# VectorE's three operations for the base row, from the fifth side group to the end of the tile's list

## The chip, the core and the metric

The kernel runs on one core of a Trainium2 chip. The metric is the device time of one execution in microseconds; less is better. The core has five engines, each with its own list of instructions and its own queue: TensorE (matrix products), VectorE, ScalarE, GpSimd, and SyncE, which here only issues DMA transfers. The lists are tied together by semaphores alone: an instruction waits for a count, and another one raises it when it has ended. No compiler orders the work; the order in each list is the order in the program.

## The reference

One transformer block on x of shape (4, 1024, 128) in float32:

```
x = x + ga * attention(layernorm(x) * (1 + ca) + sa)          # 16 heads of width 8
h = layernorm(x) * (1 + cb) + sb
probs = softmax(h @ router_w.T); p, idx = top_k(probs, 2)      # 8 experts
w = p / (p.sum(-1) + 1e-6)
x = x + gb * ((h @ expert[idx] + p) * w).sum over the two
```

The gates ga, gb and the shifts and scales come from a small table per batch. What matters here is the last line. It is computed as `base + gb * mixed`. `mixed` is the sum over all 8 experts of their output times a coefficient, which is 0 for the six not chosen. `base` is what remains: the row after attention, x1, plus gb times one number per token, `bias_w`, the sum of p times w over the two chosen experts.

## The kernel before

The 4096 tokens are 32 tiles of 128. Tiles 0 to 3 and 28 to 31 are written out, and a hardware loop of 12 rounds does two tiles a round, so tiles 4 to 27 are loop tiles; between an odd loop tile and the next even one lies the back edge. Counts of semaphores are numbers in the written-out tiles and come out of registers in the loop.

A tile t is built around the attention of tile t. TensorE computes scores in eight steps k = 0 to 7 (L801), ScalarE takes their exponentials into `probs` (L608), 16 of 128x1024 a tile, and TensorE multiplies these with the values two steps later (L819). The first operation of each step k is followed on TensorE by a side group, `side0` to `side7`, all of which share one PSUM bank, `ps_side`. They carry the other stages of other tiles, as a hand-written pipeline: layernorm and projections of tiles t+1 to t+3, the output projection and the second layernorm of tile t-1, and the router and experts of tiles t-2 and t-3. Since they share the bank, each group waits until VectorE has read what the group before it left. The ones around the change:

- `side5` (k=5) puts the products of experts 0 and 1 of tile t-2 into `ps_side`. VectorE weighs them with the router's coefficients into `weighted` (`c_weigh`, piece 0, L1264), the first weighting.
- `side6` (k=6) waits for that weighting, and transposes `xhat`, computes logits and the norms of the keys. VectorE answers with `norm_max`, `hT`, `c_logits` and `c_vals` (the reciprocal L1180 and `valsT` L1182).
- `side7` has experts 2 and 3, which VectorE weighs as piece 1, the second weighting, the last entry of VectorE's list for a tile.
- `side0` of the next tile waits for the second weighting, projects `valsT` and sums the flags. VectorE's list for a tile begins with `exact_maxima` (L1146), which loads a flag from SBUF into a register (L1149) and branches on it (L1150), and goes on with `c_x1`: x1 (L1187), its statistics (L1189, L1191), and `a_bounded` (L1144).
- `side1` waits for x1_done and bounded_done (`emptied0`) before it puts the third pair of experts in the bank.

`c_router_base` (L1242) is what the change moves: `pair_pw` (L1245, 128x2), `bias_w` (L1247, 128x1) and `base` (L1253, 128x128). Each waits for the one before it. `base` also waits for out_done of an earlier tile, and reads x1 out of one of two buffers; the next tile's `c_x1` writes that same buffer.

GpSimd has a list of its own: the two coefficients and their sum when the weights are known, `squares` of the projected queries and keys (L462), then `mix_eight` and `mix_two` for tile t-3: sums of 128x512 (L505), 128x256 (L507) and 128x128 (L511), the product with the gate (L519), and the addition of `base` (L525). For that last step it waits for base_done of tile t-3's row, which VectorE computed one tile earlier. ScalarE issues the store of the finished tile (L343) at the end of its list.

Of the kernel before, what the change touches and what calls it, by code (L numbers as in the profile page):

```python
# [51 lines left out]
def reached(eng, sem, count):  # L52

    if not isinstance(count, int) or count > 0:
        eng.wait_ge(sem, count)


def reached_apart(eng, sem, count, past, past_count):


    if not isinstance(count, int):
        count = eng.to_reg(count)
        eng.wait_ge(past, past_count)
    reached(eng, sem, count)


def spread(ap, axis, n):

    ap = ap.unsqueeze(axis)
    shape = list(ap.shape)  # L70
    shape[axis] = n
    return ap.broadcast_to(shape)


def adaln_block(nc, x, Wqkv, bqkv, Wo, bo, router_w, expert_w, c, wmod, out):
# [25 lines left out]
    with ExitStack() as ctx:  # L101
# [3 lines left out]
        def sem(name):  # L105
            return ctx.enter_context(nc.semaphore(name))
# [155 lines left out]
        ev = {n: sem(n) for n in names}  # L262
# [25 lines left out]
        def plus(eng, t, n):  # L288

            return t + n if isinstance(t, int) else eng.snap(t + n)  # L290
# [5 lines left out]
        def batch_of(eng, t):  # L296
            return t // TB if isinstance(t, int) else eng.snap(t // TB, min_val=0, max_val=B - 1)
# [777 lines left out]
        def _(dve):  # L1075
# [108 lines left out]
            def c_x1(ps, y1, ring):  # L1184
                reached(dve, ev["attn_proj_done"], y1)
                reached(dve, ev["x_gated_done"], y1)
                v.tensor_tensor(x1[:, ring, :], ps[:, 0:P], x_gated[:], ALU.add).then_inc(ev["x1_done"], 1)  # L1187
                reached(dve, ev["x1_done"], y1)
                v.bn_stats(stats2[:], x1[:, ring, :]).then_inc(ev["stats2_done"], 1)  # L1189
                reached_apart(dve, ev["stats2_done"], y1, x_rest, 16)  # L1190
                v.bn_aggr(moments2[:], stats2[:]).then_inc(ev["moments2_done"], 1)  # L1191
# [22 lines left out]
            def c_router_sorted(y1):  # L1214

                coef_before = plus(dve, y1, -1)
                reached(dve, ev["router_exp_done"], y1)
                reached(dve, ev["coef_done"], coef_before)
                v.tensor_reduce(router_sum[:], router_exp[:], AX.X, ALU.add).then_inc(ev["router_sum_done"], 1)
                reached(dve, ev["router_sum_done"], y1)  # L1220
                v.reciprocal(router_inv[:], router_sum[:]).then_inc(ev["router_inv_done"], 1)
                reached(dve, ev["router_inv_done"], y1)
                v.tensor_scalar(router_p[:], router_exp[:], router_inv[:], None, ALU.mult).then_inc(ev["router_p_done"], 1)
                reached_apart(dve, ev["router_p_done"], y1, x_rest, 16)
                v.max(top_p[:], router_p[:]).then_inc(ev["top_p_done"], 1)
# [16 lines left out]
            def c_router_base(y, y1, ring):  # L1242

                reached(dve, ev["pair_w_done"], y1)
                v.tensor_tensor(pair_pw[:], top_p[:, 0:2], pair_w[:], ALU.mult).then_inc(ev["pair_pw_done"], 1)  # L1245
                reached(dve, ev["pair_pw_done"], y1)
                v.tensor_tensor(bias_w[:], pair_pw[:, 0:1], pair_pw[:, 1:2], ALU.add).then_inc(ev["bias_w_done"], 1)  # L1247
                b = batch_of(dve, y)
                out_before = plus(dve, y1, -2)
                reached(dve, ev["bias_w_done"], y1)  # L1250
                reached(dve, ev["out_done"], out_before)
                gate = gates[:, b, :] if isinstance(b, int) else gates[:, bass.ds(b, 1), :].rearrange("p a d -> p (a d)")
                v.scalar_tensor_tensor(out=base[:, ring, :], in0=gate, scalar=bias_w[:], in1=x1[:, ring, :], op0=ALU.mult,  # L1253
                                       op1=ALU.add).then_inc(ev["base_done"], 1)

            def c_weigh(ps, y1, ring, piece):

                e0, e1 = PIECES[piece]
                mix_before = plus(dve, y1, -2)
                reached(dve, experts_done[piece], y1)  # L1260
                if piece == 0:
                    reached(dve, ev["coef_done"], y1)
                    reached(dve, ev["mix4_done"], mix_before)
                v.tensor_tensor(weighted[:, ring, e0:e1, :],  # L1264
                                ps[:, 4 * P - (e1 - e0) * D:4 * P].rearrange("p (e d) -> p e d", d=D),
                                spread(coef[:, e0:e1], 2, D), ALU.mult).then_inc(weighted_done[piece], 1)

            def gates_copied():
                dve.wait_ge(setup_pe, 5)
                step(v.tensor_copy(gates[:].rearrange("p b d -> p (b d)"), ps_side[:]))  # L1270
                assert step.n == SETUP_GATES
# [9 lines left out]
            def tile(t, parity, before, after):  # L1281
                at = {n: plus(dve, t, n) for n in range(-4, 5)}
                if isinstance(t, int) and t == 1:
                    dve.wait_ge(x_rest, 16)
                exact_maxima(t, at[1], parity)
                if before == 0:
                    a_norm_max(ps_side[:, P + NE:P + NE + 2 * J], 2)
                    a_hT(2, 3, 0)

                if after >= 1:  # L1290
                    reached(dve, ev["flags_done"], at[2])
                if before >= 2:
                    c_x1(ps_side, at[-1], parity)
                if after >= 1:
                    a_bounded(ps_side[0:1, P + R:P + R + 1], at[2], 1 - parity)

                if before >= 4:
                    c_weigh(ps_side, at[-3], parity, 2)
                if before >= 2:
                    c_x1hat(at[-1], parity)  # L1300
                if before:
                    c_save(t)

                if before == 0:
                    gates_copied()
                if before == 1:
                    weights_gated()
                if before >= 4:
                    c_weigh(ps_side, at[-3], parity, 3)
                if after >= 3:  # L1310
                    a_moments(at[3], at[4])
                if before >= 3:
                    c_router_sorted(at[-2])

                if before >= 2 and after >= 1:
                    reached(dve, ev["v_ps_done"], at[2])
                if before >= 2:
                    c_h2T(ps_side, at[-2], at[-1], parity)
                if before >= 2 and after >= 1:
                    a_values(ps_side[:, P:2 * P], at[2], 1 - parity)  # L1320
                if before >= 3:
                    c_router_weights(at[-2])

                if before < 2:
                    reached(dve, ev["v_ps_done"], at[2])
                if after >= 2:
                    a_qk(at[3])
                if before < 2:
                    a_values(ps_side[:, 2 * P:3 * P], at[2], 1 - parity)
                if after == 0:  # L1330
                    c_logits(ps_side, at[-1])
                if after >= 2:
                    a_qk_parts(at[2], at[3])
                if after >= 3:
                    a_xhat(at[3], at[4])
                if before >= 3:
                    c_router_base(at[-3], at[-2], 1 - parity)

                if before >= 3:
                    c_weigh(ps_side, at[-2], 1 - parity, 0)  # L1340
                if after == 0:
                    c_router_sorted(t - 1)
                    c_router_weights(t - 1)
                    c_vals(t)

                if after >= 2:
                    a_norm_max(ps_side[:, P + NE:P + NE + 2 * J], at[3])
                if after >= 3:
                    a_hT(at[3], at[4], 1 - parity)
                if before >= 2 and after:  # L1350
                    c_logits(ps_side, at[-1])
                if before and after:
                    c_vals(t)

                if after == 0:
                    c_x1(ps_side, t, 0)
                if before >= 3:
                    c_weigh(ps_side, at[-2], 1 - parity, 1)
                if after == 0:
                    c_x1hat(t, 0)  # L1360
                    c_router_base(t - 2, t - 1, parity)
                    c_h2T(ps_side[:, P:2 * P], t - 1, t, 2, own_ring=True)
# [222 lines left out]
```

## Time and profile before

| | |
|---|---|
| median of 3 runs | 575.02 us (574.36 to 576.14) |
| the profiled execution | 575.76 us, span 574.0 us |
| TensorE, matmul busy | 507.4 us (88%) |
| ScalarE busy | 489.5 us (85%) |
| VectorE busy | 374.4 us (65%) |
| GpSimd busy | 227.7 us (40%) |
| TensorE's granted clock, mean | 0.982 of 2.4 GHz |

The span runs from the first to the last instruction of the profiled execution; the execution's own time has a little around it. Busy shares are means over the whole. Matmuls are pipelined and their ends are modelled, so that neighbours overlap a little. In an order of time each line is a start, a duration, the engine (PE is TensorE, DVE VectorE, ACT ScalarE, POOL GpSimd; a q behind the name is the engine's queue), the line of the program and the operation; the square brackets give the idle time before it and what ended it.

### The profile page before, as it was taken

The numbers are of one execution on the slowest core, as the hardware profiler recorded it, in microseconds if no ns is written. First come the engines' busy times: TensorE is split into PE (matmuls) and PEld (weight loads), VectorE is DVE, ScalarE is ACT, GpSimd is POOL, SyncE is SP. The second block draws the span as 40 slices with busy tenths as digits, with TensorE's granted clock in tenths as the row PEclk, the third lists the DMA queues.
The fourth block names the chain that finished last, engine by engine and source line by source line (L and its number), as shares of the span: only waits on it lengthen the run. The fifth ranks groups of instructions, "written<-read, shape, count | busy, mean of one in ns | idle before, by whom it ended". The sixth has DMA issues, their size and how long they took to land.

```text
span 574.0 us, 19559 instructions
## 1 busy us (share of the span) xinstructions
PE 507.4 (88%) x6667; PEld 195.9 (34%) x6667; DVE 374.4 (65%) x1258; ACT 489.5 (85%) x574; POOL 227.7 (40%) x488
## 2 busy tenths in 40 slices
PE   6879899888888988888898888899888889988987
PEld 6523233323333332333333233333323333332326
DVE  4414566667777666777766677776667777666566
ACT  1378999888889888888988888898888899888975
POOL 1101323345454334545433444543344454334444
PEclk9688999999999999999999999999999999999999
DMA  5563323333223233322323332232333222333000
GB/s 113 150 176 85 90 73 97 94 95 86 73 70 87 74 95 94 85 71 72 86 76 95 94 82 70 76 83 78 95 93 83 69 78 83 81 99 97 21 22 19
DMA packets 83342, 48.25 MB, mean 84 GB/s; under 512 B 59608, under 2 KB 74084, under 8 KB 83300
## 3 DMA queue, kind: packets, MB, share of 16 engines
q1 hardware_dynamic: 68860, 43.30, 28.0%
q10 hardware_dynamic: 14440, 4.38, 3.5%
q8 instruction: 27, 0.44, 0.3%
q14 instruction: 15, 0.12, 0.1%
HBM read 32.78 MB, written 14.87 MB: 83 GB/s over the span
## 4 chain that ended last, share of the span: by engine, by line
PE 61%; DVE 17%; issue 10%; ACT 7%; DMA 2%; SPq 1%; DVEq 1%; ACTq 1%; POOL 0%; POOLq 0%
PE ps_attn L819 26%; PE ps_side L724 18%; PE ps_scores L801 13%; ACT probs L608 7%; DVE bias_w L1247 5%; DVE pair_pw L1245 2%; DVE qkT L1114 2%; DVE weighted L1264 2%; DVE xhat L1100 2%; DVE qk_parts L1123 1%; PE ps_side L747 1%; DMA bo_rows<-in_L_attn_bo_dram 1%; PE ps_scores L676 1%; PE ps_scores L722 1%; DVEq L1253 1%
## 5 line engine op out<-in xcount | busy, mean ns | idle before, releaser
L608 ACT ACTIVATE probs<-ps_scores 128x1024 f32<-128x1024 f32 x512 | 479.8, 1053 | 71.7 <-PE ps_scores L801 70.6
L819 PE MATMUL ps_attn<-probs,values 128*32 128x512 f32 x2048 | 273.5, 601 | 0.1
L801 PE MATMUL ps_scores<-query_stack,key_stack 32*128 32x512 f32 x1024 | 130.6, 498 | 12.8 <-issue 8.1
L801 PEld LDWEIGHTS ps_scores<-query_stack,key_stack 32*128 32x128 f32 x1024 | 49.9, 183 | 229.9 <-ACT probs L608 198.9
L454 POOL TENSOR_SCALAR var_eps<-moments 128x1 f32<-128x1 f32 x64 | 12.3, 192 | 217.8 <-DVE moments L1191 143.0
L724 PE MATMUL ps_side<-experts_in,h2T 128*32 128x256 f32 x896 | 72.3, 390 | 4.0 <-issue 0.9
L1264 DVE TENSOR_TENSOR weighted<-ps_side,coef 128x256 f32<-128x256 f32 x114 | 47.8, 419 | 37.6 <-PE ps_side L724 36.5
L819 PEld LDWEIGHTS ps_attn<-probs,values 128*32 128x32 f32 x2048 | 57.0, 110 | 25.4 <-DVE attn L1174 8.3
L724 PE MATMUL ps_side<-ident,xhat 128*32 128x128 f32 x240 | 13.0, 289 | 38.2 <-DVE weighted L1264 37.2
L505 POOL TENSOR_TENSOR mix<-weighted 128x512 f32<-128x512 f32 x29 | 37.1, 1279 | 3.7 <-ACT weighted L626 3.7
L456 POOL TENSOR_TENSOR rstd<-var_eps,minus_half 128x1 f32<-128x1 f32 x64 | 36.2, 566 | 5.4 <-POOL var_eps L454 0.2
L488 POOL TENSOR_SCALAR coef<-expert_ids,top_idf,pair_w 128x8 f32<-128x8 f32 x30 | 12.2, 406 | 64.7 <-DVE pair_w L1240 64.7
L1187 DVE TENSOR_TENSOR x<-ps_side,x_gated 128x128 f32<-128x128 f32 x31 | 9.0, 292 | 39.7 <-PE ps_side L761 38.5
L1247 DVE TENSOR_TENSOR bias_w<-pair_pw 128x1 f32<-128x1 f32 x30 | 31.0, 1032 | 1.0
L724 PEld LDWEIGHTS ps_side<-experts_in,h2T 128*32 128x32 f32 x896 | 19.1, 108 | 33.4 <-issue 32.6
L1180 DVE RECIPROCAL sums_inv<-sums 128x128 f32<-128x128 f32 x31 | 29.3, 944 | 1.8 <-DMA attnT<-a_scr 1.8
L462 POOL TENSOR_TENSOR squares<-qkT 128x256 f32<-128x256 f32 x32 | 22.8, 712 | 13.0 <-DVE qkT L1114 8.9
L1174 DVE COPY attn<-ps_attn 128x512 f32<-128x512 f32 x31 | 21.4, 692 | 7.6 <-PE ps_attn L819 6.8
L1137 DVE TENSOR_REDUCE norm_max<-ps_side 128x1 f32<-128x32 f32 x31 | 6.0, 192 | 28.4 <-PE ps_side L724 28.4
L1253 DVE SCALAR_TENSOR_TENSOR base<-gates,bias_w,x 128x128 f32<-128x128 f32 x30 | 19.1, 635 | 6.5 <-DVE bias_w L1247 6.3
L1204 DVE TENSOR_SCALAR h2T<-ps_side,mod_tab 128x128 f32<-128x128 f32 x31 | 12.7, 410 | 14.6 <-PE ps_side L747 14.1
L507 POOL TENSOR_TENSOR mix<-mix 128x256 f32<-128x256 f32 x29 | 21.1, 727 | 2.3
(185 smaller groups left out, 547.6 us busy)
## 6 DMA issues: line engine op xcount, KB each, us to landing
key_stack<-k_scr SPq DMA_DIRECT2D x128, 128.0 KB, 2.8
query_stack<-q_scr SPq DMA_DIRECT2D x125, 64.0 KB, 2.2
q_scr<-qk_parts SPq DMA_DIRECT2D x94, 64.0 KB, 1.7
k_scr<-qk_parts SPq DMA_DIRECT2D x64, 64.0 KB, 1.7
a_scr<-attn ACTq DMA_DIRECT2D x120, 18.0 KB
sums<-a_scr SPq DMA_DIRECT2D x31, 64.0 KB, 2.1
attnT<-a_scr SPq DMA_DIRECT2D x31, 64.0 KB, 2.2
out_dram<-out_all ACTq DMA_DIRECT2D x28, 64.0 KB, 2.7
```

Source lines behind the costliest of these rows:

```text
L456: g.tensor_tensor(out_[:], var_eps[:], minus_half[:], ALU.pow).then_inc(ev[done_out], 1)
L462: g.tensor_tensor(flat, src, src, ALU.mult).then_inc(ev["squares_done"], 1)
L505: g.tensor_tensor(mix4[:], weighted[:, ring, 0:4, :], weighted[:, ring, 4:8, :], ALU.add).then_inc(ev["mix4_done"], 1)
L608: nc.scalar.activation(probs[:, k % RING, g, :], ps_scores[:, slot(k, g), :], ACT.Exp, scale=SCALE)\
L724: mm = nc.tensor.matmul(dst[q:q + 32, :], stationary[:, q:q + 32], moving, start=True, stop=True, tile_position=(0, q))
L801: mm = nc.tensor.matmul(out_, key_stack[p0:p0 + 32, parity, 2 * k:2 * k + 2, :].rearrange("p j r -> p (j r)"), query_stack[p0:p0 + 32, par ...
L819: mm = nc.tensor.matmul(ps_attn[q:q + 32, :], values[:, parity, g, k, :], probs[:, k % RING, g, h * HALF:(h + 1) * HALF], start=(k == 0), ...
L1174: v.tensor_copy(attn[:].rearrange("p j r -> p (j r)"), ps_attn[:]).then_inc(ev["attn_saved"], 1)
L1180: v.reciprocal(sums_inv[:], sums[:]).then_inc(ev["sums_inv_done"], 1)
L1247: v.tensor_tensor(bias_w[:], pair_pw[:, 0:1], pair_pw[:, 1:2], ALU.add).then_inc(ev["bias_w_done"], 1)
L1253: v.scalar_tensor_tensor(out=base[:, ring, :], in0=gate, scalar=bias_w[:], in1=x1[:, ring, :], op0=ALU.mult, op1=ALU.add).then_inc(ev["bas ...
L1264: v.tensor_tensor(weighted[:, ring, e0:e1, :], ps[:, 4 * P - (e1 - e0) * D:4 * P].rearrange("p (e d) -> p e d", d=D), spread(coef[:, e0:e1 ...
```

## The change

VectorE's call of `c_router_base` in a tile is taken out from before the first weighting. In tiles 3 to 30 it stands behind the second weighting now, at the end of the tile's list. In tile 31 (`after == 0`) it stands behind the first weighting, in front of the router's work for tile 30. As `base` reads the buffer that the next tile's x1 is written to, `c_x1` gets a wait for base_done. The call for the last but one row in tile 31 (`c_router_base(t - 2, t - 1, parity)`) stays where it is. No other engine's list changes.

```diff
             def c_x1(ps, y1, ring):
                 reached(dve, ev["attn_proj_done"], y1)
                 reached(dve, ev["x_gated_done"], y1)
+                base_before = plus(dve, y1, -2)
+                reached(dve, ev["base_done"], base_before)
                 v.tensor_tensor(x1[:, ring, :], ps[:, 0:P], x_gated[:], ALU.add).then_inc(ev["x1_done"], 1)
...
                 if after >= 3:
                     a_xhat(at[3], at[4])
                 if before >= 3:
-                    c_router_base(at[-3], at[-2], 1 - parity)
-
-                if before >= 3:
                     c_weigh(ps_side, at[-2], 1 - parity, 0)
                 if after == 0:
+                    c_router_base(at[-3], at[-2], 1 - parity)
                     c_router_sorted(t - 1)
...
                 if before >= 3:
                     c_weigh(ps_side, at[-2], 1 - parity, 1)
+                if before >= 3 and after:
+                    c_router_base(at[-3], at[-2], 1 - parity)
                 if after == 0:
                     c_x1hat(t, 0)
                     c_router_base(t - 2, t - 1, parity)
```

## Rows read from the trace of the kernel before

**Rows 1.** Busy time in two windows: window, length, then busy time of each engine.

```profile
304.05:320.57 16.52, 14.92 (x211) 5.41 (x211) 11.88 (x39) 14.91 (x18) 7.26 (x15) 1.00 0.31 84
320.57:337.57 17.00, 15.04 (x210) 5.51 (x211) 11.73 (x39) 15.07 (x18) 7.37 (x15) 1.00 0.30 81
```

**Rows 2.** List of waits: who waited for whom: total us, times, longest us.

```profile
PE ps_side L724 <- DVE weighted L1264: 38.4, 26, 1.5
```

**Rows 3.** TensorE's order of time: start us, duration us, operation.

```profile
300.61 0.64 PE L724 MATMUL ps_side<-experts_in,h2T 128*32 128x256 f32 x8
...
302.04 0.51 PE L801 MATMUL ps_scores<-query_stack,key_stack 32*128 32x512 f32 x4
304.05 0.43 PE L724 MATMUL ps_side<-ident,xhat 128*32 128x128 f32 x8 [1.50 <-DVE weighted L1264]
...
309.21 0.51 PE L801 MATMUL ps_scores<-query_stack,key_stack 32*128 32x512 f32 x4
309.64 0.64 PE L724 MATMUL ps_side<-experts_in,h2T 128*32 128x256 f32 x8
```

**Rows 4.** VectorE's order of time around the three operations and the next tile's start.

```profile
300.84 0.57 DVE L1245 TENSOR_TENSOR pair_pw<-top_p,pair_w 128x2 f32<-128x2 f32 x1
301.45 1.21 DVE L1247 TENSOR_TENSOR bias_w<-pair_pw 128x1 f32<-128x1 f32 x1
302.97 0.62 DVE L1253 SCALAR_TENSOR_TENSOR base<-gates,bias_w,x 128x128 f32<-128x128 f32 x1 [0.31 <-DVE bias_w L1247]
...
305.86 0.94 DVE L1180 RECIPROCAL sums_inv<-sums 128x128 f32<-128x128 f32 x1
...
307.05 0.42 DVE L1264 TENSOR_TENSOR weighted<-ps_side,coef 128x256 f32<-128x256 f32 x1
308.50 0.29 DVE L1187 TENSOR_TENSOR x<-ps_side,x_gated 128x128 f32<-128x128 f32 x1 [1.03 <-PE ps_side L761]
...
309.33 0.15 DVE L1144 TENSOR_SCALAR bounded_int<-ps_side 1x1 int32<-1x1 f32 x1
```

**Rows 5.** VectorE's order of time in tile 3, written out.

```profile
83.84 0.16 DVE L1247 TENSOR_TENSOR bias_w<-pair_pw 128x1 f32<-128x1 f32 x1
84.04 0.35 DVE L1253 SCALAR_TENSOR_TENSOR base<-gates,bias_w,x 128x128 f32<-128x128 f32 x1
```

**Rows 6.** GpSimd's order of time in the tile of rows 3 and 4.

```profile
301.36 1.28 POOL L505 TENSOR_TENSOR mix<-weighted 128x512 f32<-128x512 f32 x1
...
304.86 0.46 POOL L525 TENSOR_TENSOR out_all<-base,mixed_gated 128x128 f32 x1 [0.19 <-POOL mixed_gated L519]
```

**Rows 7.** All of line 1264: duration ns min/median/max, first and last start us.

```profile
L1264 DVE TENSOR_TENSOR weighted<-ps_side,coef x114: 391/424/426, 84.3 to 555.4; 128x256 f32<-128x256 f32 x114
```

**Rows 8.** VectorE's queue, by line: duration ns min/median/max, first and last start us.

```profile
L1253 DVEq FUSED_REGOPS  x1: 130/130/130, 302.8 to 302.8; - x1
...
L1149 DVEq TENSOR_LOAD <-bounded_int x1: 311/311/311, 306.9 to 306.9; - x1
...
L55 DVEq EVENT_SEMAPHORE  x1: 534/534/534, 307.9 to 307.9; - x1
...
L277 DVEq ALU_OP  x1: 45/45/45, 323.4 to 323.4; - x1
...
L55 DVEq ALU_OP  x1: 40/40/40, 324.9 to 324.9; - x1
```

**Rows 9.** VectorE's order of time at the next tile's end, with the back edge.

```profile
323.57 0.42 DVE L1264 TENSOR_TENSOR weighted<-ps_side,coef 128x256 f32<-128x256 f32 x1
325.55 0.29 DVE L1187 TENSOR_TENSOR x<-ps_side,x_gated 128x128 f32<-128x128 f32 x1 [1.57 <-PE ps_side L761]
```

**Rows 10.** Chain that ended last, in order of time: start us, us, what.

```profile
326.67 0.64 PE ps_side L724 x8
```

**Rows 11.** VectorE's order of time in tile 31.

```profile
550.45 0.42 DVE L1264 TENSOR_TENSOR weighted<-ps_side,coef 128x256 f32<-128x256 f32 x1 [1.14 <-POOL mix L505]
```

**Rows 12.** ScalarE's queue: the issue of a finished tile's store.

```profile
306.36 0.39 ACTq L343 DMA_DIRECT2D out_dram<-out_all  x1
```

## The prediction

> **What bounds the kernel now.** I began with the busy time of two windows, each one round of the loop over token tiles. The first lasts 16.52 us and the second, which holds the loop's back edge, 17.00 us; TensorE is busy for 14.92 and 15.04 us of them and ScalarE for 14.91 and 15.07 us [rows 1]. TensorE's granted clock is 1.00 in both, the level of 2.4 GHz, so the clock gives nothing. Neither engine fills a round; about 1.5 us is a common hole. The list of waits names it: TensorE waited 38.4 us, 26 times, for a `weighted` of VectorE [rows 2], 1.48 us each; the 26 are the 24 loop tiles and tiles 28 and 29. In TensorE's order of time one sees the place: the scores of k=6 start at 302.04, side group 6 could follow 0.43 us later (as 309.64 follows 309.21), at 302.47, but starts at 304.05 [rows 3]. The shift to be had is thus 1.58 us here. VectorE's order of time says why: after `xhat` it runs `pair_pw` (0.57 us), `bias_w` (1.21) and `base` (0.62) before the first weighting [rows 4], though the expert products for that weighting had started at 300.61 [rows 3].
>
> These three are slow for a reason of place. In tile 3, where GpSimd has no mixing yet, `bias_w` starts at 83.84 and takes 0.16 us and `base` starts 0.20 us later and takes 0.35 [rows 5]. In the loop `bias_w` ends at 302.66 and GpSimd's first mix (301.36 plus 1.28) at 302.64 [rows 4, 6]: VectorE's small operation stands until GpSimd's large one has ended. The Trainium skill (SBUF — State Buffer, Who interferes with whom) says that a VectorE instruction with two SBUF inputs contends with a GpSimd instruction that reads SBUF, and that one of them blocks fully; by that rule the trace agrees.
>
> **The change, part by part.** *What is taken from in front of the first weighting.* It can start right after `xhat` and its expert products, at about 301.3 (products 300.61 plus 0.64), and ends 0.42 us later, 0.75 us before TensorE wants it at 302.47. It would now run beside GpSimd's first mix; it has one PSUM input, and its 114 runs lie between 391 and 426 ns wherever they fall [rows 7], so I price the contention at nothing; were it held to the mix's end at 302.64, it would end at 303.06 and give back 0.6 us a tile. The gain is 1.58 us less 0.02 for a pick-up, or from the waits 1.48 plus the 0.07 by which a matmul's modelled end overlaps the next: I take 1.55 us for each of 26 tiles, 40.3 us. ScalarE's 15 us of work fits in a round of 15.2 or more.
>
> *What the three cost at the end of the list.* I count from F, the start of side group 6 (304.05). The second weighting starts at F+3.00 (307.05) [rows 4]; from norms to weighting everything follows F. GpSimd's mixing is tied to the qk products, not to F, so its last product ends at 305.32 (304.86 plus 0.46) [rows 6], which in the new order is F+2.85. That is before the moved three start (F+3.34, one weighting's 0.34 us slot on), so they run at the short durations: `pair_pw` F+3.34, `bias_w` F+3.54, its end F+3.70. `base` followed `bias_w` by 0.31 us in this tile [rows 4], of which 0.13 is a register operation that came only after the wait [rows 8]: F+4.01. It ends at F+4.4; the added wait of `c_x1` on base_done is met by then, since x1 now starts at F+4.45 (308.50) [rows 4]. If the engine were all, the triple would be free.
>
> But VectorE's queue handles the tile's start too. Today the load of the bounded flag starts at 306.9, even before the weighting that precedes it in the list, and the queue stands ready at the waits of `c_x1` at 307.9 and waits there for 0.53 us [rows 8]. So load, register work and branch take 1.0 us and hide under the weighting and TensorE's products. In the new order the load stands behind `base`, and `base` behind the end of `bias_w`: a queue that has to wait passes nothing on. The load then starts at F+4.0, the waits come at F+5.0, and with 0.1 us for the added wait and the start, x1 runs at F+5.10 instead of F+4.45: 0.65 us later. At a back edge it is: second weighting 323.57, `bias_w` ending 0.70 later, `base` 0.20 after that, 324.47; from the loop's counter (323.4) to the last register work ahead of the waits (324.9) the queue takes 1.6 us [rows 8], so 326.1, and x1 at about 326.3 instead of 325.55 [rows 9]: 0.75 us later.
>
> Who waits for that: x1, its two statistics and `bounded_int` are one row of work, 308.50 to 309.48 [rows 4], and side group 1 on TensorE waits for x1_done and bounded_done. It starts at 309.64 [rows 3], so there is 0.16 us between, about what a signal needs: at the back edge 325.55 plus 0.98 is 326.53, and TensorE's group starts at 326.67 [rows 9, 10]. There is no slack, and the delay goes to TensorE whole: 0.65 plus 0.75, 1.40 us for each of 12 pairs, 16.8 us. Everything queued behind x1 on VectorE (third and fourth weighting, x1hat, the save of attn) shifts with TensorE's group and costs nothing more. Tile 3 pays 0.6 us and had no hole. Tiles 28 and 29 have constant counts; TensorE reaches x1 late there, and I price their delay at nothing (bounds 0 and 0.7 us each).
>
> *Tile 31.* Its first weighting waits for the mix until 550.45 [rows 11]; the three now stand after it, in front of the router's sums, the reciprocal and valsT, which the last projection needs. Short they are 0.7 us; beside GpSimd's next mixes up to 1.1 more. I take 1.0 us, lost.
>
> *Other queues.* No DMA is issued by the moved code. ScalarE's store of a finished tile is issued at F+2.3 (306.36) [rows 12] and needs GpSimd's product, which would come at F+2.85: 0.5 us of waiting in its queue, hidden under two exponentials of 0.93 us each (14.91 us for 16) [rows 1] (bound: 0.5 us a tile). `base` is needed by GpSimd one tile on.
>
> **Sum.** 40.3 less 16.8, 0.6 and 1.0 is 21.9 us. The profiled execution took 575.76 us around a span of 574.0; 575.76 less 21.9 is 553.9. The median of the runs, 575.02, is 0.74 lower: 553.1, say 553.
>
> **Rivals.** *A, the queue runs ahead (0.25).* If the load of the flag doesn't stand behind the waiting `base`, x1 keeps its time and the 16.8 us stay won: 553 less 16.8 is 536. For it: the load at 306.9 did start ahead of the weighting. Against it: it started just after the reciprocal's end (305.86 plus 0.94 is 306.80) [rows 4], when the wait of valsT was met, and `base`'s register operation came after the end of `bias_w`. The Trainium skill (Advanced Engine Details and Errata, Sequencer Loop) says that engine instructions are put in a queue and wait there for semaphores, and that the next ones can be read meanwhile. By that rule the result is this rival's; rows 4 and 8 speak against it here, as far as two waits show.
>
> *B, slower.* The triple meets GpSimd at its new place. The price is what it pays today beyond its short form: 0.42 plus 1.04 plus 0.27, 1.7 us a tile on the way to x1, which has no slack: 24 times 1.7 is 41 us on top, 594. It begins once GpSimd's mixing ends after F+3.34 instead of F+2.85, 0.5 us later than I place it, and the total is above the time of today when the extra is over 0.9 us a tile (21.9 over 24). GpSimd's chain would have to slip against the qk products, which nothing in the rows does. Chance 0.06. In a weaker form (valsT or the reciprocal is held for a last product of 0.46 us, or the weighting for the mix) it costs 0.4 to 0.6 us a tile, about 10 to 14 us: 563 to 567. Chance 0.12.
>
> *C, nothing moves (0.02):* the hole only changes place, 1.5 us lost at side group 1. That needs delays twice what I work out.
>
> **Numbers.** Forecast 553, chance 0.55, with its own range of 546 to 561 (the delay of x1 between 0.4 and 0.95 us). Range for 8 in 10: it must take in rival A and stops inside the weaker form of B: 535 to 562. About 0.3% is what a measurement here can tell from no change: faster 0.92, same 0.02, slower 0.06.
>
> **What the profile after would show.** The wait of TensorE for `weighted` gone from the list (step one); `bias_w` at 0.16 us and `base` at 0.35 (the three out of the mixing); x1 starting some 2.1 and 2.7 us after the second weighting, where it is 1.45 and 1.98 now, with TensorE waiting for `bounded_int` 0.5 to 0.8 us a tile (the queue); rounds of 15.6 and 16.2 us. If x1 keeps its distance, A holds. If `bias_w` stays near 1.2 us, B does. I am wrong altogether if side group 6 still starts late for a reason that `weighted` hides, `xhat` or the squares.

## The result, and the profile after

| | before | after |
|---|---|---|
| median of 3 runs | 575.02 us | 555.87 us (555.8 to 557.76) |
| the profiled execution, its span | 575.76, 574.0 us | 555.87, 554.0 us |
| TensorE, ScalarE busy | 507.4, 489.5 us | 510.3, 493.6 us |
| VectorE busy | 374.4 us | 329.8 us |

The changed kernel takes 0.9675 of the time (95% interval 0.9635 to 0.9714), 19 us less, where 553 us was forecast. TensorE and ScalarE do the same work; VectorE is busy 45 us less with the same operations. The list of waits of the changed kernel (who waited for whom: us in total, times, longest) has no line any more in which TensorE waits for `weighted` as in [rows 2]. In its place stands another wait of the same engine:

```profile
DVE x L1189 <- PE ps_side L761: 29.6, 24, 1.8
PEld ps_side L724 <- DVE x L1189: 27.1, 26, 1.2
PE ps_side L724 <- DVE bounded_int L1144: 19.6, 26, 1.0
```

Thus 38.4 us of waiting are gone and 19.6 us have come, once a tile in both cases. (The new wait adds two lines to the program: 1187 is 1189 now, and 1264 is 1266.) VectorE's order of time shows both halves in two tiles of the loop:

```profile
292.36 0.34 DVE L1100 TENSOR_SCALAR xhat<-x_all,moments,rstd 128x128 f32 x1
293.18 0.42 DVE L1266 TENSOR_TENSOR weighted<-ps_side,coef 128x256 f32<-128x256 f32 x1 [0.48 <-PE ps_side L724]
...
297.26 0.42 DVE L1266 TENSOR_TENSOR weighted<-ps_side,coef 128x256 f32<-128x256 f32 x1
297.59 0.15 DVE L1247 TENSOR_TENSOR pair_pw<-top_p,pair_w 128x2 f32<-128x2 f32 x1
297.78 0.16 DVE L1249 TENSOR_TENSOR bias_w<-pair_pw 128x1 f32<-128x1 f32 x1
298.17 0.35 DVE L1255 SCALAR_TENSOR_TENSOR base<-gates,bias_w,x 128x128 f32<-128x128 f32 x1 [0.23 <-DVE bias_w L1249]
299.49 0.29 DVE L1189 TENSOR_TENSOR x<-ps_side,x_gated 128x128 f32<-128x128 f32 x1 [0.97 <-PE ps_side L761]
...
312.96 0.42 DVE L1266 TENSOR_TENSOR weighted<-ps_side,coef 128x256 f32<-128x256 f32 x1
...
315.76 0.29 DVE L1189 TENSOR_TENSOR x<-ps_side,x_gated 128x128 f32<-128x128 f32 x1 [1.56 <-PE ps_side L761]
```

The first weighting waits for TensorE now and not the other way round. `pair_pw`, `bias_w` and `base` take 0.15, 0.16 and 0.35 us, as in [rows 5] and not as in [rows 4]. And x1 starts 2.23 us after the second weighting, at the back edge 2.80 us, where it was 1.45 and 1.98 us [rows 4, 9]. The brackets put x1's idle time down to TensorE, which had long been ready at the back edge; the chain that ended last, in order of time, says what really stood there (DVEq is VectorE's queue):

```profile
298.17 0.06 DVE base L1255
298.22 0.05 issue
298.27 0.38 DVEq L1149
298.65 0.03 issue
298.69 0.19 DVEq L1149
...
298.97 0.06 DVEq L1150
299.02 0.19 issue
...
299.39 0.05 DVEq L55
299.44 0.04 issue
299.49 0.30 DVE x L1189
...
300.32 0.16 DVE bounded_int L1144
300.47 0.14 issue
300.61 0.64 PE ps_side L724 x8
```

The load of the flag (L1149) starts 0.1 us behind the start of `base`; load, register work, branch and the waits of `c_x1` then take 1.2 us, and x1, `bounded_int` and TensorE's side group 1 follow one another without a gap. TensorE's own order of time has the rounds:

```profile
294.25 0.43 PE L724 MATMUL ps_side<-ident,xhat 128*32 128x128 f32 x8
...
299.42 0.51 PE L801 MATMUL ps_scores<-query_stack,key_stack 32*128 32x512 f32 x4
300.61 0.64 PE L724 MATMUL ps_side<-experts_in,h2T 128*32 128x256 f32 x8 [0.68 <-DVE bounded_int L1144]
...
309.96 0.43 PE L724 MATMUL ps_side<-ident,xhat 128*32 128x128 f32 x8
...
315.52 0.51 PE L801 MATMUL ps_scores<-query_stack,key_stack 32*128 32x512 f32 x4
316.88 0.64 PE L724 MATMUL ps_side<-experts_in,h2T 128*32 128x256 f32 x8 [0.85 <-DVE bounded_int L1144]
...
326.22 0.43 PE L724 MATMUL ps_side<-ident,xhat 128*32 128x128 f32 x8
```

From one side group 6 to the next it is 15.71 us, and 16.26 us over a back edge, against 16.52 and 17.00 us [rows 1]. Side group 1 could start 0.43 us behind its scores, as it did in [rows 3], and starts 1.19 and 1.36 us behind them.

### The profile page after: what moved, and what is told of

It reads as the page before. It is cut to its first block, busy times and chain, and to the rows that moved or that the text cites. A ratio compares the mean times of both kernels' runs of the same rounds, so it can differ in the third digit from the quotient of the medians.

```text
span 554.0 us, 19586 instructions
## 1 busy us (share of the span) xinstructions
PE 510.3 (92%) x6667; PEld 199.7 (36%) x6667; DVE 329.8 (60%) x1258; ACT 493.6 (89%) x574; POOL 228.8 (41%) x488
## 4 chain that ended last, share of the span: by engine, by line
PE 55%; DVE 18%; issue 11%; ACT 7%; DVEq 4%; DMA 3%; ACTq 1%; SPq 1%; POOL 0%; POOLq 0%
PE ps_attn L819 22%; PE ps_side L724 16%; PE ps_scores L801 11%; ACT probs L608 7%; DVE sums_inv L1180 5%; DVEq L1149 3%; DVE weighted L1266 2%; DMA attnT<-a_scr 2%; DVE stats L1191 2%; DVE x L1189 2%; DVE valsT L1182 1%; PE ps_scores L676 1%; DMA a_scr<-attn 1%; PE ps_side L747 1%; DVE norm_max L1137 1%
## 5 line engine op out<-in xcount | busy, mean ns | idle before, releaser
L724 PE MATMUL ps_side<-experts_in,h2T 128*32 128x256 f32 x896 | 71.9, 389 | 22.5 <-DVE bounded_int L1144 19.6
L1189 DVE TENSOR_TENSOR x<-ps_side,x_gated 128x128 f32<-128x128 f32 x31 | 9.0, 292 | 38.6 <-PE ps_side L761 29.6
L481 POOL TENSOR_TENSOR x_gated<-x_all,bo_gated 128x128 f32 (+1 forms) x32 | 14.8, 464 | 15.9 <-DVE bo_gated L1280 15.9
L1114 DVE TENSOR_TENSOR qkT<-ps_side,bqk_cols 128x256 f32<-128x256 f32 x32 | 13.6, 425 | 12.9 <-PE ps_side L747 5.6
L724 PE MATMUL ps_side<-hT,wqkT 128*32 128x128 f32 x480 | 19.3, 279 | 0.0
```

The lines of the kernel that those rows point to most:

```text
L724: mm = nc.tensor.matmul(dst[q:q + 32, :], stationary[:, q:q + 32], moving, start=True, stop=True, tile_position=(0, q))
```

## The experiments

All were timed beside the kernel before on the same chip; its medians there were 575.55 to 575.9 us. The figures behind "Measured" are the median, its ratio to the kernel before, and that ratio's 95% interval. Where the text speaks of the loop, it means the stretch from side group 6 of tile 3 to side group 6 of tile 28; a table further down has it for every kernel.

**Why the three are slow in the old place: GpSimd's sums cut short.** The kernel before; the first two sums get 8 columns, and the other columns are left out, so that the kernel no longer computes the block. (Two `memset` at the start, of `mix4` and `mix2`, are not shown.)

```diff
-g.tensor_tensor(mix4[:], weighted[:, ring, 0:4, :], weighted[:, ring, 4:8, :], ALU.add)
+g.tensor_tensor(mix4[:, 0, 0:8], weighted[:, ring, 0, 0:8], weighted[:, ring, 4, 0:8], ALU.add)
-g.tensor_tensor(mix2[:], mix4[:, 0:2, :], mix4[:, 2:4, :], ALU.add)
+g.tensor_tensor(mix2[:, 0, 0:8], mix4[:, 0, 0:8], mix4[:, 2, 0:8], ALU.add)
```

> The kernel before, with the three operations in their old place; GpSimd's two large sums over the experts are cut to 8 columns (the rest of the sums is left out), the third, the product with the gate and the last addition stay. It asks why the three are long in the old place. Theory (GpSimd's large sums hold them): pair_pw and bias_w near 0.15 to 0.5 us, base 0.35, the first weighting ends before TensorE is ready for side group 6, TensorE's wait of 38.4 us for weighted goes, and x1 keeps its distance of 1.45 and 1.98 us from the second weighting: 575.0 less 40 is 535 us (532 to 540). Rival (they are long for a reason of their own, their waits or the register work): 575 us, bias_w still about 1.2 us.

Measured: 542.68 us, 0.9422 (0.9387 to 0.9457) of the kernel before. The direction is the theory's; the size is 8 us short, outside its range. Its order of time (line numbers are 2 higher), VectorE in two tiles, then GpSimd in the same two:

```profile
300.62 0.57 DVE L1247 TENSOR_TENSOR pair_pw<-top_p,pair_w 128x2 f32<-128x2 f32 x1
301.22 0.16 DVE L1249 TENSOR_TENSOR bias_w<-pair_pw 128x1 f32<-128x1 f32 x1
301.59 0.35 DVE L1255 SCALAR_TENSOR_TENSOR base<-gates,bias_w,x 128x128 f32<-128x128 f32 x1 [0.21 <-DVE bias_w L1249]
...
317.31 0.60 DVE L1255 SCALAR_TENSOR_TENSOR base<-gates,bias_w,x 128x128 f32<-128x128 f32 x1 [0.31 <-DVE bias_w L1249]
```

```profile
300.47 0.70 POOL L464 TENSOR_TENSOR squares<-qkT 128x256 f32<-128x256 f32 x1
301.13 0.20 POOL L507 TENSOR_TENSOR mix<-weighted 128x8 f32<-128x8 f32 x1
...
301.69 0.57 POOL L513 TENSOR_TENSOR mixed<-mix 128x128 f32<-128x128 f32 x1
...
317.30 0.46 POOL L513 TENSOR_TENSOR mixed<-mix 128x128 f32<-128x128 f32 x1
```

`bias_w` fell from 1.21 to 0.16 us when the large sum went. `pair_pw` stayed at 0.57 us and ends at 301.19, with `squares` (301.17), which I had left in; and in the second tile `base`, 0.35 us when free, takes 0.60 beside the third sum (L513), which I had left in too. TensorE still waits 0.44 us for the weighting in that tile; 12 such tiles are 5 of the missing 8 us. So what holds them is not the large sum alone. Nor is it always VectorE that is held: in the first tile `base` starts 0.10 us before the third sum and takes its 0.35 us, and the sum takes 0.57 us instead of 0.46. A sum of 8 columns beside `bias_w` cost it nothing that shows.

**Which forms are held.** The kernel before, old place, but `pair_pw` and `bias_w` with one SBUF tensor input each.

```diff
-v.tensor_tensor(pair_pw[:], top_p[:, 0:2], pair_w[:], ALU.mult)
+v.tensor_scalar(pair_pw[:, 0:1], top_p[:, 0:1], pair_w[:, 0:1], None, ALU.mult)
-v.tensor_tensor(bias_w[:], pair_pw[:, 0:1], pair_pw[:, 1:2], ALU.add)
+v.tensor_scalar(bias_w[:], top_p[:, 1:2], pair_w[:, 1:2], pair_pw[:, 0:1], ALU.mult, ALU.add)
```

> The kernel before, the three in their old place, but pair_pw and bias_w written as tensor_scalar with one SBUF tensor input each (the weights come in as per-partition scalars); base keeps its two inputs. Theory (only forms with two SBUF inputs are held by GpSimd): pair_pw and bias_w take about 0.15 and 0.2 us; base is held until the large sum ends, 1.4 us after it began to wait or less, and ends about 0.14 us behind it; side group 6 starts 0.85 us earlier than before: 26 times 0.85 is 22 us, so 553 us (549 to 558). Rival (GpSimd holds every small operation on SBUF, whatever its form): 575 us, bias_w about 1.2 us.

Measured: 554.15 us, 0.9623 (0.9602 to 0.9644). TensorE's wait for `weighted` fell from 38.4 to 17.6 us. VectorE's order of time:

```profile
306.45 0.21 DVE L1245 TENSOR_SCALAR pair_pw<-top_p,pair_w 128x1 f32<-128x1 f32 x1
306.69 0.27 DVE L1247 TENSOR_SCALAR bias_w<-top_p,pair_w,pair_pw 128x1 f32<-128x1 f32 x1
307.18 1.22 DVE L1253 SCALAR_TENSOR_TENSOR base<-gates,bias_w,x 128x128 f32<-128x128 f32 x1 [0.21 <-DVE bias_w L1247]
```

The two in the new form run at once, beside the same `squares` and sum, and the one that still reads two SBUF tensors is now the one held, for 1.22 us. This bears out what the Trainium skill says on two SBUF inputs (SBUF — State Buffer, Who interferes with whom). Two lines of arithmetic in another form, nothing moved, bring 21 us by the medians, where the change brings 19; in the loop both bring 20.1 us.

**The new place's price by itself.** The changed kernel with the two short sums of the first experiment.

> The changed kernel, with GpSimd's two large sums cut to 8 columns as in the run with the old place (the rest of the sums is left out). In the new place the three don't meet GpSimd, so its sums should not matter: 555.9 us (553 to 558), x1 still 2.23 and 2.80 us behind the second weighting. Against the old place with short sums this gives the new place's price by itself, which my working puts at 17 to 20 us. Rival (the new place is free and the missing part of the gain is GpSimd's doing, through the first weighting, the reciprocal or valsT): 540 us or less.

Measured: 555.01 us, 0.9628 (0.9591 to 0.9666); x1 is 2.16 and 2.80 us behind the second weighting. Taking GpSimd's sums away brings the old place 33 us and the new place 1 us. So no more than 1 us of the missing gain goes with GpSimd's sums. The trace shows where that 1 us sits: with the short sums x1 comes 2.16 to 2.17 us behind the second weighting in all 12 rounds of the loop (away from the back edge), while in the changed kernel it comes 2.16 to 2.35 us behind it, and there the load of the flag takes up to 0.50 us where it takes 0.30 to 0.32 with the short sums. No GpSimd operation lies beside the long loads; why they are long is open.

**The added wait alone.**

```diff
+base_before = plus(dve, y1, -2)
+reached(dve, ev["base_done"], base_before)
```

> The kernel before plus only the added wait of c_x1 for base_done, which is long met when c_x1 comes. It measures the wait and its register work by itself. Queue theory: 0.05 to 0.15 us of the queue's time a tile, inside the 0.4 to 0.5 us for which the queue waits there anyway: 575.0 us, within 1 us. Rival (the wait is what makes x1 late after the change): 580 us or more, x1 later than 1.45 and 1.98 us after the second weighting.

Measured: 576.48 us, 1.0011 (0.999 to 1.0031); x1 1.46 and 2.08 us behind the second weighting. The medians can't tell the wait from nothing. The trace can: x1 comes 0.1 us later at each back edge, and the loop takes 420.9 us where it took 419.7.

**The queue's order: the load in front of the three.** The changed kernel, the same work, the call behind `exact_maxima` of the next tile. Its wait for out_done is for one count more; GpSimd's addition that meets it ends more than 1 us before `base` starts here too.

```diff
                 exact_maxima(t, at[1], parity)
+                if before >= 4:
+                    c_router_base(at[-4], at[-3], parity, out_back=-1)
...
-                if before >= 3 and after:
-                    c_router_base(at[-3], at[-2], 1 - parity)
```

> The changed kernel, with the three moved on by one place in VectorE's list: behind the load of the bounded flag and its branch, in front of c_x1 of the next tile. The work is the same, only the queue's order differs. Queue theory (in the changed kernel the load and the branch stand behind the wait of base): they are hidden under the second weighting again; the three start 0.9 us (1.45 at the back edge) after the second weighting, x1 1.8 and 2.35 us after it instead of 2.23 and 2.80; 12 times 0.88 is 10.5 us: 545 us (542 to 549), TensorE's wait for bounded_int about 0.3 us a tile. Rival (x1 is late because of the three's time on the engine, or the wait for base_done): the distance from the second weighting to x1 stays or grows, 555 us or more.

Measured: 547.46 us, 0.9519 (0.9475 to 0.9563), some 8 us less than the changed kernel, with the three nearer to x1 than before. In the loop it is 6.1 us; most of the rest lies ahead of side group 6 of tile 3, where it isn't the queue's order that can be at work (below). TensorE's wait for `bounded_int` is 13.2 us, from 19.6; that is 0.55 us a tile, where I expected 0.3. x1 comes 1.92 and 2.59 us after the second weighting, 0.12 and 0.24 later than I had worked out. So the order in the queue is a cause, but a smaller one than the 10.5 us I gave it: if the three's own time had been the only cause, this kernel could not have been faster. What remains, 11.2 us of the loop against the split kernel below, is the three and their waits, which now stand between the branch and x1.

**The split: the bias early, in one-input forms, and `base` late.**

```diff
                 if before >= 3:
+                    c_router_base(at[-3], at[-2], 1 - parity)
+                if before >= 3 and after == 0:
+                    c_base_row(at[-3], at[-2], 1 - parity)
+                if before >= 3:
                     c_weigh(ps_side, at[-2], 1 - parity, 0)
...
                 if before >= 3 and after:
-                    c_router_base(at[-3], at[-2], 1 - parity)
+                    c_base_row(at[-3], at[-2], 1 - parity)
```

`c_router_base` has only `pair_pw` and `bias_w` left here, in the one-input forms above, and `c_base_row` is the third operation with its waits.

> A kernel from both places: pair_pw and bias_w, in forms with one SBUF tensor input, stay in the old place in front of the first weighting; base alone stands at the end of the list (tile 31 has all three in the old place). Its wait for bias_w is long met there, so the queue should pass it at once. Queue theory: the load of the flag starts within 0.2 us of the second weighting's start, x1 is 1.45 and about 2.0 us behind that start as in the kernel before, TensorE's wait for bounded_int nearly goes (under 3 us in all), and both gains stay: 575.0 less 40 and 1 of the end is 536 us (533 to 541). Rival (base's own time, its register work and the added wait make x1 late): 550 to 556 us.

Measured: 535.48 us, 0.9293 (0.9258 to 0.9329): 40 us less than before, and the fastest kernel of this study; it computes the whole block. Three rows of VectorE's order of time and the queue's load in that tile (duration ns min/median/max, first and last start):

```profile
316.79 0.42 DVE L1268 TENSOR_TENSOR weighted<-ps_side,coef 128x256 f32<-128x256 f32 x1
317.13 0.34 DVE L1257 SCALAR_TENSOR_TENSOR base<-gates,bias_w,x 128x128 f32<-128x128 f32 x1
318.25 0.29 DVE L1189 TENSOR_TENSOR x<-ps_side,x_gated 128x128 f32<-128x128 f32 x1 [0.78 <-PE ps_side L761]
```

```profile
L1149 DVEq TENSOR_LOAD <-bounded_int x1: 314/314/314, 317.0 to 317.0; - x1
```

The load starts at 317.0, before `base` does, since `base` has nothing left to wait for, and x1 is back at 1.46 us (2.03 to 2.09 at the back edge, 0.1 of it the added wait's). In the changed kernel `base` is the same operation with the same added wait in the same place behind it; what went is the open wait, and the two short operations in front of it. TensorE waits 1.0 us for `bounded_int` in the whole run.

**Form or split?** The split kernel with the old two-input forms.

> The split kernel again (pair_pw and bias_w in front of the first weighting, base at the list's end), but with the two-input forms of the kernel before. Theory: GpSimd's large sum holds bias_w to 302.66 in the times of the kernel before; only base's 0.6 us and its register work leave the way, so side group 6 starts 0.88 us earlier than in the kernel before and x1 keeps its distance: 26 times 0.88 is 23 us, 552 us (549 to 555). That puts 16 us of the split kernel's gain on the form alone. Rival (the split does it, not the form): 535 us.

Measured: 553.95 us, 0.9631 (0.9601 to 0.9661), `bias_w` at 1.20 us. x1 did not quite keep its distance: it is 1.56 us behind the second weighting instead of 1.46, since the load of the flag takes about 0.55 us in those tiles. The form is 18 us of the split kernel's gain by the medians, and 16.1 us in the loop.

**The form in the new place.**

> The changed kernel with pair_pw and bias_w in forms with one SBUF tensor input (0.21 and 0.27 us where the old-place run had them, against 0.15 and 0.16 for the two-input forms when GpSimd is out of the way). Theory (at the new place GpSimd holds nothing, and every 0.1 us in front of base's end of waiting reaches TensorE): no gain from the form; x1 comes 0.15 us later after the second weighting, 2.38 and 2.95 us, and 24 times 0.15 is 3.6 us: 559.5 us (557 to 562). Rival (GpSimd still holds the two-input forms here for part of the tiles): less than 555.9 us.

Measured: 558.13 us, 0.9692 (0.9667 to 0.9718). The two take 0.20 and 0.27 us, and x1 comes at 2.32 and 2.97 us. What wins 21 us in one place wins nothing in the other: by the medians it is about 2 us slower than the changed kernel, with intervals that overlap; in the loop it is 3.4 us, where 3.6 was expected. Here a tenth of a microsecond in front of `base` reaches TensorE.

## Why the prediction was right, step by step

**The hole of 40.3 us**: right. Between side group 6 of tile 3 and that of tile 28 lie 25 of the 26 holes, 38.75 us by my sum. The split kernel gained 37.4 us there (from 419.7 us, 84.99 to 504.69, to 382.3 us), and its added wait costs the 1.2 us that the kernel with the wait alone lost: 38.6 us.

**The reason of place**: right that GpSimd holds the three, too narrow in naming the mixing, and the large operation. `squares` holds `pair_pw` as well. GpSimd's order of time in the changed kernel:

```profile
293.13 1.28 POOL L505 TENSOR_TENSOR mix<-weighted 128x512 f32<-128x512 f32 x1
...
296.65 0.46 POOL L525 TENSOR_TENSOR out_all<-base,mixed_gated 128x128 f32 x1 [0.19 <-POOL mixed_gated L519]
```

The first weighting, with its one input in PSUM, starts at 293.18 beside the large sum and takes its 0.42 us. Nothing of the bound of 0.6 us a tile was needed.

**The queue**: right in mechanism, a little small. I gave x1 2.10 and 2.73 us behind the second weighting; they are 2.23 and 2.80 us. The 0.13 us is in the queue's part behind `base`: it is 1.2 us in the chain, where I had taken 1.0 from [rows 8] and 0.1. Half of it is the load, 0.38 us instead of 0.31 [rows 8]. So the price was 16.8 us for the pairs and 0.6 for tile 3 by my sum, 17.4; over those rounds, hole less gain, it is 38.75 less 20.13, 18.6 us. The 38.75 is my sum's, and the split kernel with the lone wait bears it out (38.6).

**Tile 31**: 1.0 us forecast. From its first weighting to the end of the span it was 574.0 less 550.45, 23.55 us; it is 554.0 less 529.82, 24.18 us: 0.63 us.

**What the sum left out.** Side group 6 of tile 3, which TensorE reaches without a wait in either kernel, starts at 85.86 instead of 84.99 us. Over all the kernels that start lies anywhere between 82.40 and 86.00 us, though their work up to there differs in little: the three operations of tile 3, the added wait, two `memset`. So I don't put the 0.9 us down to the change; what makes the start differ is open. It also means that a comparison of two kernels by their medians may carry up to some 3 us of this, and the loop between the two side groups is the cleaner measure (us, from the profiled executions):

| kernel | side group 6 of tile 3 | of tile 28 | between |
|---|---|---|---|
| before | 84.99 | 504.69 | 419.7 |
| changed | 85.86 | 485.43 | 399.6 |
| short sums, old place | 84.43 | 472.98 | 388.6 |
| one-input forms, old place | 84.58 | 484.17 | 399.6 |
| short sums, new place | 86.00 | 484.65 | 398.7 |
| added wait alone | 83.88 | 504.81 | 420.9 |
| load in front of the three | 82.71 | 476.22 | 393.5 |
| split | 83.62 | 465.91 | 382.3 |
| split, two-input forms | 82.40 | 480.81 | 398.4 |
| one-input forms, new place | 84.87 | 487.82 | 403.0 |

The account of the span is then: start 0.9 more, the loop to tile 28 20.1 less, the end 0.7 less, together 20.0 less, where I had 21.9. The last 0.7 us of the difference to 555.87 is my step from the profiled execution to the median: the new kernel's profiled execution is its median.

**Rival A** (the queue runs ahead) is out: the load stands 0.1 us behind the start of `base` in the chain and 0.6 us behind the end of the second weighting, where it used to start ahead of that weighting, and 536 us is what one gets when `base` has no open wait, not with the changed kernel. The Trainium skill (Advanced Engine Details and Errata, Sequencer Loop) has an engine instruction pushed into a queue, where it waits for its semaphores. From that one would expect the load to run while `base` waits; the trace doesn't agree (298.27 against 298.17), and the measurement decides. In the loop tiles a register operation of `base` stands in between, so that they alone would not settle it. Tile 28 is written out and has none, and there too the load starts only behind the start of `base`, 0.01 us behind it:

```profile
488.84 0.16 DVE L1249 TENSOR_TENSOR bias_w<-pair_pw 128x1 f32<-128x1 f32 x1
489.04 0.35 DVE L1255 SCALAR_TENSOR_TENSOR base<-gates,bias_w,x 128x128 f32<-128x128 f32 x1
```

```profile
L1149 DVEq TENSOR_LOAD <-bounded_int x1: 309/309/309, 489.1 to 489.1; - x1
```

**Rival B** is out in both forms: GpSimd's last product ends at 297.11 in the first tile above, the three start at 297.59, and the reciprocal and valsT keep 0.94 and 0.29 us. **Rival C** is half of the truth: about half of the hole did change its place.

## What to carry to other kernels

Before moving an operation off a critical path, look at why it is long. One with two SBUF inputs beside GpSimd may be long only through its form; changing the form can bring as much as the move. And count the engine's queue with the engine: an instruction that must wait for its neighbour, put in front of register loads, branches or a loop's end, makes all of these late, although it costs the engine itself next to nothing; move the part that waits to a place where its wait is already met when the queue comes to it, as the split kernel did with `base`.

## What the runs showed of the hardware

- Short operations in a row are held one after another, each by the GpSimd operation that is then running: `pair_pw` until `squares` ended, `bias_w` until the large sum did, `base` until the next. Where `base` started 0.10 us ahead of a GpSimd sum, it was the sum that grew, from 0.46 to 0.57 us. From the start of the first to the first weighting it is 2.67 us (300.84 to 303.51) where tile 3 has 0.64 (83.66 to 84.30).
- `tensor_scalar` on 128x1 with its other operands as per-partition scalars out of SBUF ran beside GpSimd in 0.21 and 0.27 us where `tensor_tensor` took 0.57 and 1.21. In the changed kernel the reciprocal of 128x128 ran from 296.07 beside GpSimd's product with the gate and its last addition in 0.94 us, as in the kernel before, where nothing of GpSimd's lay beside it.
- VectorE's queue took 1.0 us from the start of the load of one value to the waits behind its branch (306.9 to 307.9, [rows 8]), 1.2 us to x1 in the changed kernel (298.27 to 299.49), and 0.6 us more at the loop's back edge (x1 at 2.80 instead of 2.23 us). In the changed kernel the load took 0.30 to 0.50 us.
- The load of the flag ran ahead of an operation that only waited for a busy engine (317.0 against `base` at 317.13 in the split kernel), and not ahead of one whose semaphore was still open (tile 28, above).
